# Distance attention: the query's offset as three bf16 parts of one sum per batch, and extra products fetched four steps late

## The reference

```python
D_MODEL, N_HEAD, BATCH, NTOK, A2LEN = 64, 8, 2, 256, 255
wq = scl * normal(N_HEAD * D_MODEL, D_MODEL + 1)   # last column is the bias, here 0
wv = scl * normal(N_HEAD * D_MODEL, D_MODEL + 1)
wk = 0.005 * ones(N_HEAD, D_MODEL)
a2a = permutation(NTOK)[:A2LEN]
```

## Time and profile before

| | us |
|---|---|
| median of 3 runs (1448.35 to 1449.5) | 1448.46 |
| the profiled execution | 1447.95 |
| its span, first to last instruction | 1446.2 |
| `distance_attend`, offset group of block 0 to last step's product | 1021.8 to 1301.8 |
| TensorE busy in the span | 1110.9 (77%) |
| VectorE busy | 892.9 (62%) |
| ScalarE busy | 769.1 (53%) |
| GpSimd busy | 141.1 (10%) |

### The profile page before, as it was taken

One profiled execution on the slowest core, in us unless ns is written; L12 is line 12 of the kernel. 1 busy time (PEld: TensorE's weight loads), 2 busy tenths in 40 slices (PEclk: granted clock), 3 DMA queues, 4 the chain that ended last, 5 costly groups with the idle time before them and its releaser, 6 DMA issues. The chain is left out here.

```text
span 1446.2 us, 27934 instructions
## 1 busy us (share of the span) xinstructions
PE 1110.9 (77%) x11498; PEld 648.6 (45%) x11498; DVE 892.9 (62%) x1929; ACT 769.1 (53%) x1076; POOL 141.1 (10%) x159
## 2 busy tenths in 40 slices
PE   6667955382778979955999999979899999997240
PEld 3456944381534444441333333365444555667220
DVE  0476457647891177765675555564777979953624
ACT  0451323121207643348999999922687978962020
POOL 0006302202001200000000000010000000001424
PEclk9778987555557979956999999969899999995575
DMA  6100000022000000000000000010000000002021
GB/s 143 28 1 1 4 4 9 7 30 46 3 1 1 1 0 1 1 2 3 1 2 1 2 1 1 2 39 1 2 2 2 2 2 2 2 2 66 12 45 27
DMA packets 42315, 18.18 MB, mean 13 GB/s; under 512 B 37504, under 2 KB 41138, under 8 KB 41934
## 3 DMA queue, kind: packets, MB, share of 16 engines
q1 hardware_dynamic: 40462, 15.32, 5.0%
q0 software_dynamic: 1728, 1.08, 0.4%
HBM read 12.88 MB, written 3.48 MB: 11 GB/s over the span
## 5 line engine op out<-in xcount | busy, mean ns | idle before, releaser
L2398 ACT ACTIVATE pt_PT<-ps 128x1024 f32<-128x1024 f32 x288 | 266.1, 1111 | 5.8 <-PE ps L2468 5.4
L3417 ACT ACTIVATE da_AD<-ps,da_NX 128x1024 f32<-128x1024 f32 x214 | 222.4, 1123 | 41.0 <-PE ps L3498 40.4
L3498 PE MATMUL ps<-da_AD,dw_win 128*32 128x256 f32 x4080 | 230.7, 380 | 8.9 <-DVE da_AD L3369 8.9
L3369 DVE TENSOR_SCALAR da_AD<-da_QH,da_XG,da_XH 128x1024 f32<-128x1024 f32 x296 | 217.5, 811 | 13.8 <-PE ps L3498 13.4
L3498 PEld LDWEIGHTS ps<-da_AD,dw_win 128*32 128x32 f32 x4080 | 128.0, 110 | 108.2 <-DVE da_AD L3369 19.8
L2434 PE MATMUL ps<-pt_PT,pa_V 128*32 128x512 f32 (+3 forms) x1536 | 154.9, 497 | 8.3 <-DVE pt_Yc L2375 3.2
L2382 DVE TENSOR_TENSOR pt_PT<-pt_PT,pt_keep 128x512 f32<-128x512 f32 x128 | 84.3, 690 | 61.5 <-ACT pt_PT L2398 60.3
L2468 PE MATMUL ps<-pt_QT,pt_KT 12*128 12x512 bf16 (+3 forms) x768 | 80.3, 334 | 3.4 <-DVE pt_KT L2340 0.5
L2434 PEld LDWEIGHTS ps<-pt_PT,pa_V 128*32 128x32 f32 x1536 | 38.8, 109 | 64.5 <-issue 63.3
L2007 ACT ACTIVATE mt_act<-ps 128x342 f32<-128x342 f32 (+1 forms) x66 | 30.1, 455 | 54.0 <-PE ps L2062 54.0
L2062 PE MATMUL ps<-mt_XF,ew_w 64*128 64x342 f32 (+1 forms) x132 | 54.2, 494 | 0.9 <-ACT mt_WT L1993 0.8
(11 more groups left out here) (766 smaller groups left out, 2098.7 us busy)
## 6 DMA issues: line engine op xcount, KB each, us to landing
em_xs<-in_x_dram SPq DMA_DIRECT2D x2, 1152.0 KB, 9.2
em_xs<-in_x_dram SPq DMA_DIRECT2D x2, 1024.0 KB, 13.5
cp_xbuf<-ci_zero SPq DMA_DIRECT2D x1, 672.0 KB
cp_XS<-cp_xbuf SPq DMA_DIRECT2D x8, 84.0 KB, 2.2
cp_ybuf<-cp_YS SPq DMA_DIRECT2D x8, 84.0 KB, 2.1
ew_win<-in_L_ffn_w_dram SPq DMA_DIRECT2D x2, 320.0 KB
em_WS<-in_L_tok_W_dram SPq DMA_DIRECT2D x8, 72.0 KB
la_blk<-la_scratch SPq DMA_DIRECT2D x8, 64.1 KB
```

The source lines that it names most:

```text
L2398: nc.scalar.activation(PT[:, n % RING, 2 * i:2 * i + 2, :], ps[:, b0:b0 + 2, :], ACT.Exp, scale=SCALE).then_inc(exp_ok, 1)
L3369: nc.vector.tensor_scalar(AD[:, j % RING], QH[:, b], XG[:, b, s:s + 1], XH[:, b, s:s + 1], ALU.max, ALU.subtract).then_inc(ad_dve, 1)
L3417: nc.scalar.activation(AD[:, j % RING], QA, ACT.Abs, bias=NX[:, b, s:s + 1]).then_inc(ad_act, 1)
L3498: ins = nc.tensor.matmul(o, D.win[:, int(by[j] == "D"), hp, 15 - m:47 - m], AD[:, j % RING, hp], start=False, stop=m == (14 if (k, q) == ( ...
```

## The change

The offset depends on the batch and the query only; it is the same number for every key of VectorE. So it is computed once per batch as a sum S (one row for each head of each pair) and then spread over the rows by a product with a 0/1 matrix.

- Four more extra products S0 to S3 (two per batch, each two f32 products with `D.own`, now 66 columns wide) make S; VectorE copies them to `S32`.
- GpSimd splits S32 into three bf16 parts, `R3`, on partitions 0-1, 32-33 and 64-65: six dependent operations per batch on 1024 elements a partition (four copies with a change of type, two subtractions); the first two are on 66 partitions.
- The offset group of a block is now two bf16 products of 66 x 128 by 66 x 512 (`offsets`). In block 0, where the parts are not there yet, it runs with zeros, and the true one is added after step 22. ScalarE's exponential of block 0 moves behind it, from step 19 to step 27, that of block 4 from 83 to 91.
- Extra products: S0, S1, Q0, Q1, S2, S3, V0 to V7, after steps 2, 6, ... 54. `XLAG` is 4 in place of 1, for the gathers of the weighing too, and the weighing moves to steps 68, 73, 78 and 83.
- One constant more (`c_rows`, 66 x 128, 14 DMAs in place of 13), one more copy on GpSimd in `fill`; `own` and its constant are 66 columns wide in place of 128; one memset on GpSimd ahead of the stage's first operation.

```diff
+OWN = 66
...
+for k in range(3):
+    for h in range(2):
+        own[64 * h:64 * h + 64, 32 * k + h] = -1.0
+        rows[32 * k + h] = maxed & (half == h)
...
-    EXTRAS = ("Q0", "Q1") + tuple(f"V{j}" for j in range(8))
-    XFIRST, XEVERY, XLAG = 2, 4, 1
+    EXTRAS = ("S0", "S1", "Q0", "Q1", "S2", "S3") + tuple(f"V{j}" for j in range(8))
+    XFIRST, XEVERY, XLAG = 2, 4, 4
-    WEIGH = {68 + 2 * hp: hp for hp in range(4)}
+    WEIGH = {68 + 5 * hp: hp for hp in range(4)}
+    EXPS = {16 * e + (27 if e in (0, 4) else 19): e for e in range(7)}
...
+                    elif EXTRAS[x][0] == "S":
+                        nc.vector.tensor_copy(S32[:, j // 2, 2 * (j % 2):2 * (j % 2) + 2],
+                                              pairs_of(2 + x % 2)[0:OWN]).then_inc(s_sb, 1)
...
-                        if n - 1 in WEIGH:
-                            gather(WEIGH[n - 1])
+                        if n - XLAG in WEIGH:
+                            gather(WEIGH[n - XLAG])
...
-                    act.wait_ge(red_ps, 16 * e + 16)
+                    act.wait_ge(red_ps, 16 * e + 16 if e else 23)
...
+                nc.gpsimd.memset(R3[:, 0], 0.0).then_inc(nil_ok, 1)
+                pool.wait_ge(nil_ok, 1)
...
+                link = Chain(pool, part_ok)
+                gp = nc.gpsimd
+                for b in range(B):
+                    pool.wait_ge(s_sb, 2 * b + 2)
+                    link(gp.tensor_copy(R3[:, b], S32[:, b]))
+                    link(gp.tensor_tensor(S32[:, b], S32[:, b], R3[:, b], ALU.subtract))
+                    for r in (slice(32, 34), slice(64, 66)):
+                        link(gp.tensor_copy(R3[r, b], S32[r, b]))
+                    r = slice(64, 66)
+                    link(gp.tensor_tensor(S32[r, b], S32[r, b], R3[r, b], ALU.subtract))
+                    gp.tensor_copy(R3[r, b], S32[r, b]).then_inc(own_ok, 1)
...
+                def offsets(e, start):
+                    for i in range(2):
+                        ins = nc.tensor.matmul(pairs_of(4 * (e % 2) + i), D.rows[:], R3[:, e // 4, 2 * i:2 * i + 2],
+                                               start=start, stop=not start, skip_group_check=True)
+                    return ins
...
-                        if e == 4:
-                            pe.wait_ge(q_sb, 8)
-                        for hp in range(4):
-                            nc.tensor.matmul(pairs_of(4 * (e % 2) + hp // 2)[:, hp % 2], D.own[:, hp], QH[:, b, hp],
-                                             start=True, stop=False, skip_group_check=True)
+                        if e == 0:
+                            pe.wait_ge(nil_ok, 1)
+                        else:
+                            pe.wait_ge(own_ok, b + 1)
+                        offsets(e, True)
...
+                    if n == 22:
+                        pe.wait_ge(own_ok, 1)
+                        ins = offsets(0, False)
```

More of the change, by code:

```diff
@@ L115, in constants @@
     c["c_window"] = win
-    own = (np.arange(128)[:, None] // 64) == half[None, :]
+    own, rows = np.zeros((128, OWN), np.float32), np.zeros((OWN, 128), np.float32)
     maxed = np.array([MAXED[4 * (r % 16) + r // 32] for r in range(128)])
-    c["c_own"] = -(own & maxed[None, :]).astype(np.float32)
+    for k in range(3):
+        for h in range(2):
+            own[64 * h:64 * h + 64, 32 * k + h] = -1.0
+            rows[32 * k + h] = maxed & (half == h)
+    c["c_own"], c["c_rows"] = own, rows
     ex = np.zeros((64, 8 * 170), np.float32)
@@ L3142, in __init__ @@
         self.one, self.win = sb("one", [128, 47]), sb("win", [128, 2, 4, 47])
-        self.same, self.own = sb("same", [128, 128]), sb("own", [128, 4, 128])
+        self.same, self.own = sb("same", [128, OWN]), sb("own", [128, 4, OWN])
+        self.rows32, self.rows = sb("rows32", [OWN, 128]), sb("rows", [OWN, 128], BF16)
         self.XD = sb("XD", [65, B, 4, 128])
@@ L3149, in __init__ @@
         self.scaled = K.sem("dw_scaled")
-    LOADS = 13
+    LOADS = 14
     def load(self, nc, sp, A):
@@ L3168, in load @@
         sp.dma_start(self.same[:], A["c_own"]).then_inc(self.in_, 16)
+        sp.dma_start(self.rows32[:], A["c_rows"]).then_inc(self.in_, 16)
     def fill(self, nc, pool):
@@ L3181, in fill @@
                               ).then_inc(self.filled, 1)
+        pool.wait_ge(self.filled, 5)
+        nc.gpsimd.tensor_copy(self.rows[:], self.rows32[:]).then_inc(self.filled, 1)
         for b in range(B):
-            pool.wait_ge(self.filled, 5 + b)
+            pool.wait_ge(self.filled, 6 + b)
             nc.gpsimd.tensor_copy(self.VR[:, b, :, :, 64], bc(self.half8[:], 4)).then_inc(self.filled, 1)
@@ L3200, in select @@
         if step == 0:
-            dve.wait_ge(self.filled, 7)
+            dve.wait_ge(self.filled, 8)
             dve.wait_ge(self.in_, 16 * self.LOADS)
@@ L3213, in select @@
             nc.vector.tensor_tensor(self.bq[:], self.wq[:, :, 64], self.wrec[:], ALU.mult).then_inc(self.scaled, 1)
-            nc.vector.tensor_tensor(self.own[:], bc(self.same[:], 4), bcl(self.wabs[:], 128), ALU.mult
+            nc.vector.tensor_tensor(self.own[:], bc(self.same[:], 4), bcl(self.wabs[:], OWN), ALU.mult
                                     ).then_inc(self.scaled, 1)
@@ L3281, in distance_attend @@
         PP = sb("PP", [128, 4, 4, SELP])
+        S32, R3 = sb("S32", [OWN, B, 4, SELP]), sb("R3", [OWN, B, 4, SELP], BF16)
         rec, rec8 = sb("rec", [128, 2, 2]), sb("rec8", [128, 2, 8])
@@ L3411, in _ @@
                         act.wait_ge(qa_ok, 2)
-                    if j == first[n] and n % 16 == 3 and n >= 16:
-                        exps(n // 16 - 1)
+                    if j == first[n] and n in EXPS:
+                        exps(EXPS[n])
                     if by[j] == "A":
@@ L3421, in _ @@
             def _(pool):
+                nc.gpsimd.memset(R3[:, 0], 0.0).then_inc(nil_ok, 1)
+                pool.wait_ge(nil_ok, 1)
                 pool.wait_ge(x_ok, 1)
                 nc.gpsimd.tensor_scalar(XH[:], XG[:], 0.5, 1.0, ALU.mult, ALU.mult).then_inc(xh_ok, 1)
-                pool.wait_ge(D.filled, 7)
+                pool.wait_ge(D.filled, 8)
                 for b in range(B):
@@ L3446, in extra @@
                         pe.wait_ge(q_sb, 4 + 2 * int(EXTRAS[x - 2][1]) + 2)
+                    elif EXTRAS[x - 2][0] == "S":
+                        pe.wait_ge(s_sb, int(EXTRAS[x - 2][1]) + 1)
                     else:
@@ L3453, in extra @@
                                                    XG[0:64, 1], start=True, stop=True)
+                    elif kind == "S":
+                        if j == 0:
+                            pe.wait_ge(D.scaled, 4)
+                        for a in range(2):
+                            hp = 2 * (j % 2) + a
+                            ins = nc.tensor.matmul(pairs_of(2 + x % 2)[0:OWN, a], D.own[:, hp], QH[:, j // 2, hp],
+                                                   start=True, stop=True)
                     else:
@@ L3498, in _ @@
                             ins = nc.tensor.matmul(o, D.win[:, int(by[j] == "D"), hp, 15 - m:47 - m], AD[:, j % RING, hp],
-                                                   start=False, stop=m == (14 if (k, q) == (3, 3) else 15),
-                                                   skip_group_check=True)
+                                                   start=False, stop=False, skip_group_check=True)
+                    if n == 22:
+                        pe.wait_ge(own_ok, 1)
+                        ins = offsets(0, False)
                     ins.then_inc(red_ps, 1)
```

1 line of the change is left out of this document (added).

## The result

The changed kernel took 1432.13 us (median of 4 runs, 1429.12 to 1437.87) against 1448.98 (4 runs). A second comparison of the same two programs with more runs gave 0.9896 (0.9868 to 0.9923).

The account below looks back on a forecast made before the run. TensorE was taken to bound the stage, losing time to VectorE's late tiles; savings and costs summed to -17.2 us, GpSimd's splitting gave back 8.4, so -8.8 from 1448.46, stated as 1439.5 us, range 1430 to 1445.

Parts of the forecast that it names:

- The bound: In the 128 steps of `distance_attend`, TensorE bounds; it stood 8.9 us for VectorE's tiles, VectorE 15.4 for V products.
- Offset group: At the start of each block, two bf16 products take 0.62 us instead of 1.92, saving 1.30 in blocks 1 to 7.
- The clock at the start: At step 0, TensorE idles beforehand and runs one step at half speed: +1.7 us, bounds 0 and 3.5.
- GpSimd's splitting: In each batch, GpSimd's six operations cost VectorE their whole 8.6 us; 8.4 us in all reach TensorE.
- the extra products: In blocks 0 to 3, each holds TensorE 1.05 us; S0 to S3 add 4.2 us.
- the ring's lead of 6.9: Up to step 31, VectorE's lead of 6.9 us hides the first splitting chain and leaves nothing for the second.
- The range: For the whole kernel, 1430 to 1445 us stated; the forecast's own, from clock and offset group, 1435 to 1443.
- Rival A: In the splitting, GpSimd's work costs VectorE nothing: 1431.3 us, 1430 with no low clock; chance 0.20.
- Rival B: At step 16, batch 0's chain is shut out and late, TensorE waits, +9.8: 1441 us, up to 1444; chance 0.18.
- D: In the whole stage, the producers already bound it, so no gain comes: within 2 us of before; chance 0.06.
- C: At steps 16 and 64, both chains are late, each wait leaving the low clock: +22.4, 1453.7 us; chance 0.06.

Follow-up runs that it names:

- lag_only: The kernel before with only fetch lag four and the weighing at steps 68, 73, 78, 83, offset still f32: loop 264.11 us, ratio 0.9929 to the kernel before.
- no_split: The changed kernel without GpSimd's twelve splitting operations and the waits for them, so the offset is not added: loop 261.17 us, median 1430.74.
- warm: The changed kernel with four unread f32 products added ahead of the first offset group, before step 0: loop 262.30 us, stage 289.39.
- split_twice: The changed kernel with GpSimd's six operations per batch repeated on scratch tiles behind the real ones, nothing waiting for them: loop 275.48 us.
- halves: The changed kernel with each batch's splitting done in two halves, the first as soon as S0 (S2) is fetched: loop 268.87 us.
- lag2: The changed kernel with a fetch lag of two steps, the weighing's steps unchanged: loop 272.10 us.

## Why the prediction was right, and where its sum was off

- *The bound*: right. TensorE stalled behind VectorE's waits for products; lag_only shows that these stalls alone are worth 12.3 us. Without GpSimd's work the blocks were given as 33.7, 33.2, 63.1 for 2 and 3, 64.7 for 4 and 5, 28.4 and 36.5; no_split has 34.25, 33.37, 63.76, 65.09, 28.30 and 36.40. The sum of the forecast was 259.6, the run's 261.17. Most of the 1.6 us is the extra products: one cost 1.19 us in block 2 of no_split ((33.08 - 27.77 - 0.54) / 4), not 1.05, and there are 14. Block 5 was expected at 28.4 and took 30.42, since the last weighing lies in it.
- *Offset group*: 0.62 forecast, 0.54 measured. *The clock at the start*: 1.7 forecast, 1.84 in the changed kernel, and warm shows that it is the clock. Step 0 came 0.3 nearer to the first group, 0.4 were forecast.
- *GpSimd's splitting*: this term was mis-sized, 8.4 us forecast and 3.0 measured by no_split. Two parts of it failed. VectorE's loss was put at 17.2 us, each operation's whole length, and is 12.6 by the two rows of nine tiles (13.23 and 12.52 us, where such a row takes 6.60 and 6.58 alone); split_twice added 12.0. And "the ring's lead of 6.9 hides the first chain and nothing is left for the second" was wrong: the first chain cost 2.05 us in block 0, and by the second VectorE was some three steps ahead again, since its tiles lost nothing while GpSimd's cast was shut out, and two offset groups and three products had held TensorE back in the meantime; the second cost 0.9, in block 2. So block 1, which was to take about 40 us from its group, took 33.38. My sum took VectorE's whole time to step 31, as if it had never waited for the ring after the first 0.6 us, and added it to the end of step 31. VectorE's first tile began at 1019.03, so that step should have ended 78.5 us later; it ended after 72.9.
- *The range*: the forecast's own range was given as 1435 to 1443, and 1432.13 lies below it. It moved the clock and the offset group only (their bounds make it 1436.2 to 1444.7) and held the splitting at 8.4, for which the text itself had bounds of 0 and 17.2. The measured time lies in the stated range because that was widened for the rivals. In the loop 268.0 us were forecast and 264.16 measured: 5.4 too much for the splitting and 1.6 too little for the rest.
- *Rival A* (nothing lost) came nearest in time, 1431.3, but its mechanism is refuted: tiles beside GpSimd last 1.52 to 2.63 us. A part of the agreement is chance, since the median fell by 16.9 us and the loop by 12.3. *Rival B*'s mechanism is shown in halves, and its wait at step 16 did not occur in the changed kernel. *D* is refuted by lag_only. *C* did not occur; the price that it put on the low clock after such a wait, 1.7, was 2.4 in halves (block 1 took 35.77 us instead of 33.38).
- The Trainium skill, page "SBUF — State Buffer", section "Who interferes with whom", has the two engines exclude each other for a whole operation. The trace agrees with the exclusion (a cast of 0.61 us that lasts 6.84), though here the cast stood for nine operations and not for one. As a price the rule is too high here: a tile beside a cast of 1.03 us lost 0.72.

Left open: whether the gap itself lets GpSimd in at the start of a chain, and why a stream of tiles without one shuts it out there, while once it is in the two engines go one for one, although the tiles then follow each other just as closely.

## What to carry to other kernels

When a producer must also fetch results of the engine that it feeds, fetch them late, by at most as many steps as the buffer between them is deep: the price of fetching early is not the fetch but the lead that is lost with it. Two steps were enough here as long as nothing else took time from VectorE, and with GpSimd's work beside it four were better than two. Work given to GpSimd is not free if VectorE's tiles go from memory to memory beside it, as here (1024 elements in 0.73 us); give VectorE a lead to eat from, or give copies to ScalarE, and put a dependent chain where a long delay does no harm. Removing products just ahead of a loop can leave TensorE at the low clock for the loop's first steps; look at the granted clock there before counting the saving.

## What the runs showed of the hardware

- A GpSimd cast of 512 elements, 0.61 us alone, lasted 6.84 beside an unbroken stream of nine VectorE tiles and ended 0.47 us behind them; VectorE's tiles were not slowed by it (6.58 us). All nine opening casts that were done at once stand at a gap of 0.02 us or more in VectorE's stream, all thirteen that were shut out at none.
- Once in, GpSimd's operations and VectorE's tiles went one for one, and a tile lasted 2.63 us beside a subtraction, 0.80 alone.
- TensorE at the low clock kept to it through three steps' first 3.6 us though it was busy without a gap; three products and the offset group, ended 0.91 us before step 0, did not help; three or four with the group behind them that ran up to step 0 did.
- After a wait of 5.28 us in the middle of the loop TensorE's granted clock was 0.50 for more than 4 us (halves), and the next three steps took 7.36 us instead of 5.39. Of two waits of 3.48 and 3.49 us in lag2 the first was followed by 0.50, the second by 1.00.
- What follows the stage, in code that no edit touched, took 132.7 to 137.3 us from one profile to the next, and the stage's start lay between 1002.7 and 1015.0, while the loop under study repeated within 0.04 us.
